# A linear recurrence whose output is summed in PSUM onto the turned x, with its gate in the weights

## What is computed

```
h   = layernorm(x) * (1 + ca[b]) + sa[b]
u   = B h ;  s[t] = lambda * s[t-1] + gamma * u[t]        (complex, 64 states)
y   = Re(C s) + D h
x   = x + ga[b] * y                                       # the part that is changed
h2  = layernorm(x) * (1 + cb[b]) + sb[b]
x   = x + gb[b] * (shared_expert(h2) + sum of the top-2 routed experts)
```

## Time and profile before

| | |
|---|---|
| median of 3 runs | 557.93 us (557.34 to 558.0) |
| span of the profiled execution | 556.3 us |
| PE busy | 488.8 us (88%) |
| DVE busy | 432.2 us (78%) |
| ACT busy | 348.2 us (63%) |
| POOL busy | 334.6 us (60%) |
| chain that ended last | PE 68%, DVE 14%, POOL 6%, ACT 6%, issue 4% |

### The profile page before, as it was taken

How to read it: one execution, slowest core, us unless ns; L and a number is a source line. 1 busy time by engine, 2 the same in 40 slices (tenths; PEclk the granted TensorE clock), 3 DMA queues, 4 the chain that set the end, 5 groups by cost and what they waited for, 6 DMA issues and landing times.

```text
span 556.3 us, 11701 instructions
## 1 busy us (share of the span) xinstructions
PE 488.8 (88%) x4017; PEld 307.6 (55%) x4017; DVE 432.2 (78%) x1172; ACT 348.2 (63%) x1002; POOL 334.6 (60%) x259
## 2 busy tenths in 40 slices
PE   5650048999999999999989999999999999999997
PEld 3320014467777777543457777777644445667775
DVE  6999999889999886556899999985545688366665
ACT  4971004689999997532579999998647526533332
POOL 5860006999999997776889999995010277420000
PEclk9885559999999999999989999999999999999999
DMA  8400002311111112000041111111000000000000
GB/s 290 165 0 1 1 1 78 69 37 41 39 37 33 39 41 86 2 1 0 2 113 41 40 35 35 41 39 39 1 3 0 0 1 1 1 0 20 20 20 20
DMA packets 14880, 19.93 MB, mean 36 GB/s; under 512 B 2362, under 2 KB 8996, under 8 KB 14692
## 3 DMA queue, kind: packets, MB, share of 16 engines
q1 hardware_dynamic: 14532, 19.08, 12.7%
q10 hardware_dynamic: 288, 0.08, 0.1%
HBM read 8.94 MB, written 1.05 MB: 18 GB/s over the span
## 4 chain that ended last, share of the span: by engine, by line
PE 68%; DVE 14%; POOL 6%; ACT 6%; issue 4%; DMA 1%; DVEq 0%; POOLq 0%; ACTq 0%
PE psT L1396 11%; PE psQK L1469 9%; PE psO L1591 6%; PE psO L1523 5%; PE psQK L1798 5%; PE psS L1571 5%; DVE vst L990 3%; DVE vAB L994 3%; PE psO L1396 3%; PE psS L1870 3%; PE psQK L1605 3%; PE psS L1707 3%; PE psO L1870 2%; PE psQK L1730 2%; PE psO L1709 2%
## 5 line engine op out<-in xcount | busy, mean ns | idle before, releaser
L526 ACT ACTIVATE prob<-psS,nmx 128x128 f32<-128x128 f32 x256 | 89.9, 377 | 18.0 <-DVE nmx L1135 18.0
L819 POOL TENSOR_TENSOR rn<-ssq,half 128x16 f32<-128x16 f32 x32 | 93.0, 2907 | 8.0 <-DVE ssq L1121 7.9
L811 POOL TENSOR_TENSOR ra<-ra,rb 128x512 f32<-128x512 f32 x64 | 80.9, 1284 | 1.0 <-DVE rb L1103 0.9
L666 POOL TENSOR_TENSOR rst<-mv,half 128x4 f32<-128x4 f32 x24 | 25.7, 1070 | 73.8 <-DVE mv L922 63.6
L1469 PE MATMUL psQK<-wqkv,hsA 128*128 128x512 f32 x128 | 62.0, 604 | 1.0 <-DVE hsA L1084 0.6
L526 ACT ACTIVATION_READ_ACCUMULATOR prob<-psS,nmx 128x1 f32 x256 | 55.6, 217 | 0.0
L1100 DVE TENSOR_TENSOR ra<-psQK,rope 128x512 f32<-128x512 f32 x64 | 43.9, 686 | 10.2 <-PE psQK L1469 9.7
L827 POOL TENSOR_TENSOR qkn<-ra,rn 128x512 f32<-128x512 f32 x32 | 49.0, 1532 | 2.5
L1103 DVE TENSOR_TENSOR rb<-psQK,rope 128x512 f32<-128x512 f32 x64 | 43.6, 681 | 0.0
L647 ACT ACTIVATE gel<-psQK 128x512 f32<-128x512 f32 x32 | 19.1, 597 | 37.5 <-PE psQK L1798 37.5
L1114 DVE TENSOR_REDUCE ssq<-sq 128x8 f32<-128x512 f32 x64 | 41.1, 677 | 1.6 <-ACT sq L466 1.3
(11 more groups left out here) (240 smaller groups left out, 1204.1 us busy)
## 6 DMA issues: line engine op xcount, KB each, us to landing
vAB<-vAB SPq DMA_DIRECT2D x62, 128.0 KB, 2.2
wqkv<-in_wqkv SPq DMA_DIRECT2D x2, 768.0 KB, 8.4
big<-in_x SPq DMA_DIRECT2D x4, 256.0 KB, 4.5
ropeb<-in_rope SPq DMA_DIRECT2D x1, 1024.0 KB, 6.5
big<-in_ew SPq DMA_DIRECT2D x2, 512.0 KB, 4.7
wmod<-in_wmod SPq DMA_DIRECT2D x2, 384.0 KB, 6.0
out<-big SPq DMA_DIRECT2D x3, 256.0 KB, 2.3
w<-in_w SPq DMA_DIRECT2D x2, 341.0 KB
```

The lines of the kernel that those rows point to most:

```text
L526: act.activation(prob[:, k, :], psS[:, hb, c * P:(c + 1) * P], ACT.Exp, bias=nmx[:, k:k + 1], accum_out=sums[:, n % 2, k:k + 1]).then_inc( ...
L811: pool.tensor_tensor(o, o, rb[:, r], ALU.add).then_inc(s["sum_" + name], 1)
L819: pool.tensor_tensor(rn[:, :], ssq[:, :], half[:, :], ALU.pow).then_inc(s["rn_ready"], 1)
```

## The change

The output of the recurrence is made by tokens instead of by channels. For each group, `lru_direct` now turns `x_cm` into the statistics bank of `late_ln(1, g)` (four transposes), and adds D h as four 128-token products onto it; `lru_back` adds its two parts as four products each. The gate ga is multiplied into the three matrices ahead of it (`wlg`, by POOL, from a row in `osb`), so the bank holds x + ga y. `lru_mixed` then takes the statistics straight from the bank and copies the bank to `big[:, 4]`; `x_cm` is not written any more, and neither `late_t1(1, g)` nor the second turn at L1843 is left. The shared expert's product starts its bank itself, and DVE adds it to `big[:, 4]` instead of copying.

Both gates' rows are now made by one call, `gate_rows`, in the last MLP (l = 1, g = 1) after `out_proj`: four products in place of two, a copy of 512 columns on ACT in place of 256. POOL's four products for `wlg` stand ahead of `ln_rstd(late_ln(0, 0))`. On DVE the order changes: `lru_mixed(g)` comes one scan later than before.

```diff
@@ stat_bank: late_ln(1, 0..3) in psT0, psS[:, 1], psQK[:, 0], psT0
-                bank = (psT0[:, :], psQK[:, 0, :], psT0[:, :], psS[:, 1, :], psS[:, 1, :], psT0[:, :], psS[:, 1, :],
+                bank = (psT0[:, :], psQK[:, 0, :], psT0[:, :], psS[:, 1, :], psT0[:, :], psS[:, 1, :], psQK[:, 0, :],
                         psT0[:, :])[n - 4 * NG]
@@ ScalarE, last MLP
                     mlp_gelus(l, g)
                     if l and g == 1:
+                        act.wait_ge(s["gb_mm"], 4)
+                        act.activation(osb[:, :], psQK[:, 1, :], ACT.Copy).then_inc(s["gb_ready"], 1)
                         act.wait_ge(s["tabs_phase"], 1)
                         act.activation(tcos, tcos, ACT.Sin, scale=TWO_PI).then_inc(s["tabs_ready"], 1)
@@ ScalarE, recurrence
             for g in range(2, NG):
-                if g == NG - 1:
-                    act.wait_ge(s["gb_mm"], 2)
-                    act.activation(osb[:, 0:2 * P], psQK[:, 1, P:3 * P], ACT.Copy).then_inc(s["gb_ready"], 1)
                 ln_norm(late_ln(0, g))
                 lru_out(g)
             for g in range(NG):
+                act.wait_ge(s["xmid_ready"], g + 1)
                 ln_norm(late_ln(1, g))
@@ GpSimd, ahead of ln_rstd(late_ln(0, 0))
+            pool.wait_ge(s["gb_ready"], 1)
+            for b in range(B):
+                pool.tensor_tensor(wlg[:, b, 0:1, :], wlru[:, 4:5, :], gate_row(0, b, 1), ALU.mult).then_inc(s["wl_ready"], 1)
+                pool.tensor_tensor(wlg[:, b, 1:3, :], wcs[:, :, :], gate_row(0, b, 2), ALU.mult).then_inc(s["wl_ready"], 1)
@@ VectorE
             def lru_mixed(g):
-                b = bof(g)
+                n = late_ln(1, g)
                 dve.wait_ge(s["y_done"], g + 1)
-                dve.scalar_tensor_tensor(out=x_cm[:, gsl(g)], in0=psQK[:, 0, :], scalar=mod[:, 1, GA, b:b + 1],
-                                         in1=x_cm[:, gsl(g)], op0=ALU.mult, op1=ALU.add).then_inc(s["xmid_ready"], 1)
+                ln_stats(n, stat_bank(n))
+                dve.tensor_copy(big[:, 4, gsl(g)], stat_flat(n)).then_inc(s["xmid_ready"], 1)
...
             lru_scan(0)
             lru_products(1)
-            lru_mixed(0)
             lru_scan(1)
             lru_products(2)
-            ln(late_ln(1, 0))
-            lru_mixed(1)
+            lru_mixed(0)
             lru_scan(2)
             lru_products(3)
-            ln(late_ln(1, 1))
+            lru_mixed(1)
+            lru_scan(3)
             lru_mixed(2)
-            lru_scan(3)
             shared_hidden(0)
-            ln(late_ln(1, 2))
             lru_mixed(3)
-            ln(late_ln(1, 3))
             shared_hidden(1)
...
-                dve.tensor_copy(big[:, 4, gsl(g)], (psT0, psT1)[g % 2][:, :]).then_inc(s["ey_used"], 1)
+                dve.tensor_tensor(big[:, 4, gsl(g)], big[:, 4, gsl(g)], (psT0, psT1)[g % 2][:, :], ALU.add).then_inc(s["ey_used"], 1)
@@ TensorE, last MLP
+            def gate_rows():
+                pe.wait_ge(s["z_ready"], NG + 1)
+                pe.wait_ge(s["mod_fin"], 2)
+                for k in range(2):
+                    for b in range(B):
+                        mm(psQK[:, 1, (k * B + b) * P:(k * B + b + 1) * P], mod[:, 1, (GA, GB)[k], b:b + 1].to_broadcast([P, P]),
+                           ident[:, :], start=True, stop=True).then_inc(s["gb_mm"], 1)
...
                     if g == 1:
                         out_proj(l, 3)
+                        if l:
+                            gate_rows()
...
+                    if l and g == 1:
+                        pe.wait_ge(s["gb_ready"], 1)
                     for j, (o, m) in enumerate(HCH):
@@ TensorE, recurrence
+            def lru_sum(g, bank, left, right, last):
+                for k in range(TPG):
+                    i = mm(bank[:, k * P:(k + 1) * P], left[:, k * P:(k + 1) * P], wlg[:, bof(g), right, :],
+                           start=False, stop=last, skip_group_check=True)
+                return i
             def lru_direct(g):
-                if g:
-                    pe.wait_ge(s["xmid_ready"], g)
-                else:
-                    pe.wait_ge(s["ln_norm"], TPG * (late_ln(0, 1) + 1))
-                mm(psQK[:, 0, :], wlru[:, 4, :], lru_hn[g], start=True, stop=False)
+                bank = stat_flat(late_ln(1, g))
+                pe.wait_ge(s["ln_norm"], TPG * (late_ln(*((0, 2), (0, 3), (0, 1), (1, 0))[g]) + 1))
+                if g == NG - 1:
+                    pe.wait_ge(s["xmid_ready"], 1)
+                pe.wait_ge(s["x_mixed"], NG + g + 1)
+                for k in range(TPG):
+                    mm(bank[:, k * P:(k + 1) * P], x_cm[:, g * GW + k * P:g * GW + (k + 1) * P], ident[:, :],
+                       is_transpose=True, start=(k == 0), stop=(k == TPG - 1), skip_group_check=True)
+                pe.wait_ge(s["wl_ready"], 2 * (bof(g) + 1))
+                lru_sum(g, bank, lru_hn[g], 0, False)
             def lru_back(g):
+                bank = stat_flat(late_ln(1, g))
                 pe.wait_ge(s["lru_m1"], g + 1)
-                mm(psQK[:, 0, :], wcs[:, 0, :], lru_cos[g % 2], start=False, stop=False)
+                lru_sum(g, bank, lru_cos[g % 2], 1, False)
                 pe.wait_ge(s["lru_m2"], g + 1)
-                mm(psQK[:, 0, :], wcs[:, 1, :], lru_sin[g % 2], start=False, stop=True).then_inc(s["y_done"], 1)
+                lru_sum(g, bank, lru_sin[g % 2], 2, True).then_inc(s["y_done"], 1)
...
             lru_drive(1)
-            expert_gates()
             lru_back(0)
             ln_t2(late_ln(0, 3))
             lru_drive(2)
-            late_t1(1, 0)
             lru_direct(1)
             lru_back(1)
             lru_drive(3)
-            late_t1(1, 1)
             lru_direct(2)
@@ TensorE, shared expert
-                pe.wait_ge(s["xmid_ready"], g + 1)
-                for k in range(TPG):
-                    mm((psT0, psT1)[g % 2][:, k * P:(k + 1) * P], x_cm[:, g * GW + k * P:g * GW + (k + 1) * P], ident[:, :],
-                       is_transpose=True, start=(k == 0), stop=(k == TPG - 1), skip_group_check=True)
+                if g == 0:
+                    pe.wait_ge(s["xmid_ready"], NG)
+                    pe.wait_ge(s["ln_norm"], TPG * (late_ln(1, NG - 1) + 1))
+                elif g == 1:
+                    pe.wait_ge(s["ln_out"], late_ln(1, NG - 1) + 1)
```

More of the change, by code:

```diff
@@ L99, in program @@
         wcs = sb("wcs", [P, 2, P])
+        wlg = sb("wlg", [P, B, 3, P])
         wsh = sb("wsh", [P, 2, 256])
@@ L197, in program @@
             rt_mm sig_done pairs_ready better_ready comb_ready sh_mm sh_act sh_h ey_done eh_mm eh_act ey_used acc_done
-            gb_mm gb_ready wg_ready out_ready""".split()
+            gb_mm gb_ready wl_ready wg_ready out_ready""".split()
         s = {n: sem(n) for n in names}
@@ L859, in _, with gate_row @@
                     phase_cosine()
+            def gate_row(k, b, count):
+                return osb[:, (k * B + b) * P:(k * B + b + 1) * P].unsqueeze(1).to_broadcast([P, count, P])
+            pool.wait_ge(s["gb_ready"], 1)
+            for b in range(B):
+                pool.tensor_tensor(wlg[:, b, 0:1, :], wlru[:, 4:5, :], gate_row(0, b, 1), ALU.mult).then_inc(s["wl_ready"], 1)
+                pool.tensor_tensor(wlg[:, b, 1:3, :], wcs[:, :, :], gate_row(0, b, 2), ALU.mult).then_inc(s["wl_ready"], 1)
             for g in range(NG - 1):
@@ L891, in gate @@
             def gate(b, count):
-                return osb[:, b * P:(b + 1) * P].unsqueeze(1).to_broadcast([P, count, P])
-            pool.wait_ge(s["gb_ready"], 1)
+                return gate_row(1, b, count)
             pool.wait_ge(s["ld_moe"], 16 * 5)
@@ L1669, in attention, with late_t1 @@
                     out_high(l, 0)
-            def late_t1(kind, g):
-                if kind == 0:
-                    pe.wait_ge(s["x_mixed"], NG + g + 1)
-                else:
-                    pe.wait_ge(s["xmid_ready"], g + 1)
-                ln_t1(late_ln(kind, g), x_cm[:, gsl(g)])
+            def late_t1(g):
+                pe.wait_ge(s["x_mixed"], NG + g + 1)
+                ln_t1(late_ln(0, g), x_cm[:, gsl(g)])
+            def gate_rows():
[5 more added lines that the diff above has]
+                           ident[:, :], start=True, stop=True).then_inc(s["gb_mm"], 1)
             for l in range(LAYERS):
@@ L1718, in _ @@
                     if g == NG - 2 and l + 1 == LAYERS:
-                        late_t1(0, 0)
+                        late_t1(0)
                         pe.wait_ge(s["zmid"], NG * LAYERS)
-                        late_t1(0, 1)
+                        late_t1(1)
                     elif g == NG - 1 and l + 1 == LAYERS:
                         ln_t2(late_ln(0, 0))
-                        late_t1(0, 2)
+                        late_t1(2)
                         ln_t2(late_ln(0, 1))
@@ L1746, in _ @@
             pe.wait_ge(s["ld_moe"], 16 * 5)
[L1748 to L1754, removed]
             def lru_drive(g):
@@ L1762, in lru_drive @@
```

(29 more changed lines are left out.)

1 line of the change is left out of this document (removed).

## The result

The changed kernel takes 561.17 us (median of 12 runs, 558.36 to 561.50), the kernel before beside it 558.13 (12 runs). The ratio of the means is 1.0049, 95% interval 1.0038 to 1.0059. It is slower; the forecast was 558.6, and 561.17 lies above its range, which ended at 560.6. The span of its profiled execution (a run of 561.40) is 559.6, against 556.3.

The account below looks back on a forecast made before the run. The prediction took PE as the bound nearly everywhere, with a few waits for other engines. Last MLP +3.32, recurrence -1.68 and shared expert -0.98 gave +0.66 us on 557.93, so 558.6; range 556.9 to 560.6.

Parts of the forecast that it names:

- Part 1: Last MLP: the gates' rows delay ACT's copy and norm by 3.62 us; recurrence starts 3.32 late (bounds 2.9 to 3.5).
- The sum: Whole kernel: +3.32 - 1.68 - 0.98 = +0.66 us, time 558.6, bounds 557.3 to 560.5.
- Rival (b): Last MLP: PE's new 2.5 us stand lowers the clock for the w1 products, 1.8 us more, 560.4; chance 0.09.
- Part 2: Recurrence: less PE work and fewer waits, 31.8 us against 33.48, a gain of 1.68 (bounds 0.41 to 2.0).
- four close hand-offs: Recurrence: four hand-offs to PE lie within 0.2 us, so any miss costs.
- (c): Recurrence: norms reach PE late by 0.2 to 0.5 us each, gain falls to 0.6, time 559.7; chance 0.14.
- (d): Recurrence sums: narrow products onto a bank cost 2.5 times as much, time 573; chance 0.01.
- (a): Last MLP: the stall is off the path or made up by later waits, time 555.3; chance 0.11.
- Part 3: Shared expert: removed turns save 0.49 us each in groups 1 and 3, gain 0.98 (bounds 0.5 to 1.5).

Follow-up runs that it names:

- fill_stand: The changed kernel plus ten products that nobody reads in PE's queue, where it stands still in the last MLP: 559.62 us, 1.0031 times before.
- early_pool: `rows_early`, with POOL's last expert product (second batch's gated weights) made to wait until DVE has weighed the experts: 556.50 us, 0.9972 times before.
- rows_mid: The changed kernel with `gate_rows` moved between the two halves of `out_proj`: 557.77 us, 0.9988 times before.
- rows_alone: The kernel before with only the gates' rows made as in the changed kernel, recurrence and shared expert as they were: 563.13 us, 1.0091 times before.
- rows_early: The changed kernel with `gate_rows` moved ahead of `out_proj` in the last MLP: 557.37 us, 0.9991 times before.
- before_fill: The kernel before plus eight products of no use in PE's queue at its stand near 280 us, second transformer block: 558.06 us, 0.9997 times before.

## Why the prediction was wrong, step by step

**Part 1, the stall: right.** The copy was to start at 420.55 and the norm to be 3.62 late. Counted from `out_proj`'s start the copy comes at 420.56 and the norm 3.64 late. PE was to stand 2.5; it stood 2.29. With the clock held (`fill_stand`), the recurrence starts 3.34 late, counted from `out_proj`'s start in both profiles (446.44 - 415.98 against 443.16 - 416.04); the forecast was 3.32. POOL's four `wlg` products ran from 428.80 to 431.04 and its next norm began at 436.68: they cost nothing.

**The clock: the step that failed, the larger of two.** The sum put the products behind the new stand at full clock; they ran at half of it, and 1.53 was missing. Rival (b) had the mechanism, the place and nearly the price (1.8; measured 1.5 to 1.7). What was wrong is its chance, 0.09, and the two reasons for it. That "PE is dense before that stand" was no protection: it was busy for 8.50 of 8.80 us before the stand and the clock fell. That "no row shows it after dense work" was false of the trace it was said of: the fall at 282 in the kernel before stands behind a stand of 1.88 us that follows a block of matmuls (busy for 3.00 of 3.00 us from 276). The argument rested on one stretch, in the first layer, where PE had stood for 2.47 us; the row to look for was the granted clock behind every stand of about 2 us. Of the Trainium skill's page "TensorE: Matmul & The Clock Gate", the section HAM oscillation says that an engine which idles between bursts is throttled again. The traces here agree in part: it happened after dense work too and behind stands shorter than the waits of the page's example, but not behind every one.

**Part 2, the recurrence: right.** 1.59 gained where 1.68 was forecast; the sums of four cost 0.89 (forecast 0.90), the four close hand-offs held, and the marked waits left are the two of group 0 (0.52 and 0.43). Rivals (c) and (d) are out, (a) with them: the stall was on the path.

**Part 3, the shared expert: mis-sized, 0.31 in place of 0.98.** Two things took the rest.
- DVE's L1350 is in the path from the hidden product of group 2 to those of group 3. It ends 0.08 after POOL's L912 in the changed kernel (493.51 and 493.43). In the kernel before, DVE's L1347 took 0.51 beside the same POOL product and ended 0.09 after it (489.78 and 489.69). What group 1's turn saved brought DVE there earlier, but not POOL, whose three products count from DVE's earlier work: the 0.39 went into the wait. The prediction named DVE as the bound of group 2 and didn't ask what bounds DVE. `early_pool` shows it: 0.23 without POOL's product, and 19.84 from the first weighted to the first routed product in place of 20.52. The Trainium skill says in "SBUF — State Buffer", Who interferes with whom, that a `tensor_scalar` can take a port pair that DVE and GpSimd share and that the one which comes second waits for the whole instruction; 0.90 with and 0.23 without the product agree.
- A weighted product without its turn ahead of it costs more itself: in groups 1 and 3, where it now follows PE's wait, and in group 0, where it follows the router's products, the sixteen instructions took 2.03 to 2.05. In the kernel before, behind a turn, and here in group 2, which PE enters without a pause, they took 1.95. That is 0.08, 0.10 and 0.10.

0.98 less 0.39 and less 0.28 is the 0.31.

**The sum.** The forecast's own +0.66 becomes +1.33 with part 3 as measured, and `fill_stand`, which has all but the clock, measures 1.64 more than before in the median, 1.3 in the span and 1.43 from `out_proj` to the first routed product. The clock adds 1.53, which makes 2.9 to 3.0 of the 3.04 between the medians. Neither miss alone leaves the range: 558.6 with the 1.53 is 560.1, and with the 0.67 it is 559.3. The range failed because it took in rival (b) and the low end of part 3 each alone; together they are 558.6 + 1.8 + 0.48, which is 560.9 and outside it.

**What stays open.** Two of the twelve runs of the changed kernel took 558.36 and 558.58, the other ten 560.92 to 561.50. A stand that isn't followed by a fall, as at 280, would explain 1.5 of it, and 558.46 is the fastest of `fill_stand`; no profile fell on such a run. What decides whether a stand is followed by a fall, these runs don't settle. It isn't its length alone: behind the 1.88 at 280 the clock fell in three profiles of eight, and behind the 2.47 of the earlier trace rows it fell in three (before, `rows_mid`, `rows_alone`, 0.57 from 35 to 39) and not in `rows_early` and `before_fill` (1.00).

## What to carry to other kernels

Work that is hung ahead of another engine's queue costs what that queue feeds; look for a place where its input is ready earlier, since the same four products cost 0.9 us ahead of `out_proj` and 3.3 behind it. When a change makes PE stand, read the granted clock behind every stand of that length in the trace, dense work before it or not, and put the half-clock time into the sum; look in more than one profile, since the same stand can have the fall in one execution and not in the next. When an instruction leaves an engine's chain, ask of the engine that is then the bound what it waits for itself, and add up the bad ends that can come together.

## What the runs showed of the hardware

- The granted clock fell to 0.50 (1.2 of 2.4 GHz) for about 3 us behind a stand of 2.29 us that follows dense work, in all three profiles that had it, and cost 1.5 to 1.7 us. Behind a stand of 1.10 us, in the one profile that has it there, it stayed at 1.00. Behind 1.88 us it fell in three profiles of eight; it cost 1.48 us on the spot, of which 0.93 was left 138 us later. Ten products that nobody reads, in the stand of 2.29 us, kept it at 1.00.
- A DVE `tensor_scalar` of 128x128 took 0.23 us by itself, and 0.51 and 0.90 beside a POOL product, according to how much of that product was left; both times it ended 0.08 to 0.09 after it. The `tensor_reduce` ahead of it took 1.21 us with a POOL product under way (L1349 of the changed kernel) and 1.21 without (`early_pool`).
